# A graph attention layer on one core: packing the adjacency four columns to a word before it is searched

## The reference

```python
h = jnp.maximum(_layernorm(x, axis=-1), 0.0)
h = jnp.einsum('ni,hif->hnf', h, W)
s1 = jnp.einsum('hnf,hf->hn', h, a1)
s2 = jnp.einsum('hnf,hf->hn', h, a2)
scores = jax.nn.leaky_relu(s1[:, :, None] + s2[:, None, :], negative_slope=0.2)
scores = jnp.where(adj[None] > 0, scores, -9e15)
att = jax.nn.softmax(scores, axis=-1)
out = jnp.einsum('hnm,hmf->hnf', att, h)
x = x + elu(transpose and reshape of out to (6144, 512))
```

## Time and profile before

| | |
|---|---|
| median of 3 runs | 944.34 us (942.68 to 944.92) |
| profiled execution, its own time | 940.65 us |
| its span | 938.7 us |
| VectorE busy | 781.5 us, 83% |
| TensorE busy | 625.6 us, 67% |
| ScalarE busy | 467.2 us, 50% |
| GpSimd busy | 451.0 us, 48% |
| FIND_INDEX8, L327, 240 of them | 337.3 us |
| ACTIVATE of the adjacency, L430, 96 of them | 266.2 us |
| granted TensorE clock, mean | 0.853 |

### The profile page before, as it was taken

How to read it: one execution, slowest core, us unless ns; L and a number is a source line. 1 busy time by engine, 2 the same in 40 slices (tenths; PEclk the granted TensorE clock), 3 DMA queues, 4 the chain that set the end, 5 groups by cost and what they waited for, 6 DMA issues and landing times. The chain is left out here.

```text
span 938.7 us, 9287 instructions
## 1 busy us (share of the span) xinstructions
PE 625.6 (67%) x2178; PEld 363.9 (39%) x2178; DVE 781.5 (83%) x1767; ACT 467.2 (50%) x707; POOL 451.0 (48%) x1004
## 2 busy tenths in 40 slices
PE   0115766665766766657753695598957896978894
PEld 0003433433433434434432453355534453545442
DVE  3799999999989989989987675377958697989995
ACT  0217888888888888888881110012312231223322
POOL 3404444444444344344442666745767476746730
PEclk9967798899889889897895797789969798989897
DMA  8635999999999999999941666756868588868862
GB/s 290 236 134 194 395 402 414 413 414 418 415 413 419 414 411 413 415 415 408 407 157 47 192 183 170 228 155 199 241 208 266 167 262 258 261 211 255 278 218 91
DMA packets 86011, 269.53 MB, mean 287 GB/s; under 512 B 16129, under 2 KB 24321, under 8 KB 81218
## 3 DMA queue, kind: packets, MB, share of 16 engines
q1 hardware_dynamic: 66194, 203.13, 55.8%
q0 software_dynamic: 19760, 65.78, 24.0%
HBM read 243.49 MB, written 25.37 MB: 286 GB/s over the span
## 5 line engine op out<-in xcount | busy, mean ns | idle before, releaser
L327 DVE FIND_INDEX8 places<-ones,sb_adj_rows 128x8 uint32<-128x392 int32 (+6 forms) x240 | 337.3, 1413 | 0.0
L430 ACT ACTIVATE positive<-sb_adj_rows 128x3088 bf16<-128x3088 int32 (+3 forms) x96 | 266.2, 2773 | 0.0
L491 PE MATMUL psH<-sb_W,normedT 128*128 128x512 f32 x384 | 246.3, 734 | 1.7 <-ACT normedT L451 1.7
L1060 PE MATMUL psO<-weighted_h,ident 128*128 128x512 f32 x276 | 171.5, 710 | 25.1 <-issue 25.1
L832 POOL DMA_INDIRECT nodes<-table,column x138 | 140.8, 1020 | 66.1 <-issue 40.4
L483 PE MATMUL psT<-ident,normed 128*128 128x128 f32 x192 | 37.8, 329 | 199.7 <-ACT normed L444 199.7
L837 POOL DMA_INDIRECT nodes<-table,list_column x109 | 111.0, 1018 | 76.3 <-DVE list_column L945 45.0
L986 DVE TENSOR_TENSOR weighted_h<-nodes,psW 128x2048 f32<-128x2048 f32 (+5 forms) x74 | 139.5, 1925 | 0.0
L533 POOL TENSOR_TENSOR node_sum<-node_sum,h_rows 128x512 f32<-128x512 f32 x48 | 61.1, 1274 | 153.0 <-ACT h_rows L460 153.0
L1066 PE MATMUL psO<-weighted_h,to_row 128*128 128x512 f32 x218 | 127.0, 668 | 6.6 <-issue 4.4
L492 PEld LDWEIGHTS psS<-sb_Wa,normedT 128*128 128x128 f32 x384 | 84.6, 220 | 114.9 <-issue 114.9
(11 more groups left out here) (155 smaller groups left out, 852.7 us busy)
## 6 DMA issues: line engine op xcount, KB each, us to landing
sb_adj_rows<-in_adj_dram SPq DMA_DIRECT2D x36, 1344.0 KB, 13.4
sb_adj_rows<-in_adj_dram SPq DMA_DIRECT2D x36, 960.0 KB, 9.3
sb_adj_rows<-in_adj_dram SPq DMA_DIRECT2D x36, 576.0 KB, 6.6
table<-h_rows SPq DMA_DIRECT2D x48, 260.0 KB, 9.6
sb_x_rows<-in_x_dram SPq DMA_DIRECT2D x48, 256.0 KB, 9.8
x_part<-in_x_dram SPq DMA_DIRECT2D x19, 512.0 KB
out_dram<-result SPq DMA_DIRECT2D x19, 512.0 KB
sb_adj_rows<-in_adj_dram SPq DMA_DIRECT2D x10, 720.0 KB, 9.9
```

The costliest lines, as they stand in the source:

```text
L327: ins = nc.vector.max_index(places[:, t % 2, 8 * s:8 * s + 8], sb["ones"][:, 0:8], adj_rows[:, u, a:b + SENTINELS])
L430: ins = nc.scalar.activation(positive[:, cols], adj_rows[:, u, cols], ACT.Relu, accum_out=sb["sums"][:, t, half:half + 1])
L491: nc.tensor.matmul(psH[:, t % 2], normedT[:, t % 2, kc], sb["W"][:, kc], start=(kc == 0), stop=(kc == KC - 1))
L1060: nc.tensor.matmul(psO[:, o, i], sb["ident"][:], weighted_h[:, u % 2, q], start=a, stop=False)
```

## The change

ScalarE's pass over the adjacency writes something that is then used. The 6144 columns of a row are taken as four stretches of 1536 (WORDS). pack(t, b) writes stretch b as byte b of 1536 words (packed, two buffers), so a word holds columns w, 1536 + w, 3072 + w and 4608 + w. Byte 0 is written as 4 in place of 1, so that a word has an exact value in f32; the plan weighs its count by 0.25. VectorE then works on 1536 words a tile: greatest finds the eight greatest words of each segment (nc.vector.max, MAX8), search finds their places (max_index against these words), with 16, 8 or 4 segments as before. GpSimd takes the found words apart: for each of the four bytes it tests whether it is over 0 and makes the falling number of its column, so there are four times as many candidates, and rank works on arrays four times as wide. Sentinels, their memsets and the table of lengths are gone; a tile's adjacency is loaded in one DMA issue of whole rows. Its buffer is free when ScalarE has packed it.

VectorE's order for tile t is now moments(t + 2), scale(t + 1), greatest(t), then the searches of all segments with the ranks of t - 1 between them. greatest(t) waits for checked to reach t + 1, which the last pack of tile t sets. ScalarE's pack(t) waits, from tile 3 on, for the search of t - 2. The orders of ScalarE and GpSimd keep their places.

```diff
-SENTINELS = 8
+PACK = 4
+WORDS = N // PACK
...
 
-    marks = [N * k * k // (shares * shares) for k in range(shares + 1)]
+    def edges(w):
+        return sum(math.sqrt(b * WORDS + w) - math.sqrt(b * WORDS) for b in range(PACK))
+    marks = [0] + [min(range(WORDS + 1), key=lambda w: abs(edges(w) - edges(WORDS) * k / shares)) for k in range(1, shares)] + [WORDS]
...
-                for s, (lo, hi) in enumerate(segments):
-                    nc.gpsimd.memset(sb["lens"][t][:, 8 * s:8 * s + 8], float(hi - lo))
-                    nc.gpsimd.memset(sb["bases"][t][:, 8 * s:8 * s + 8], float(N + 1 - lo))
+                for b in range(PACK):
+                    for n, (lo, hi) in enumerate(segments):
+                        nc.gpsimd.memset(sb["bases"][t][:, b, 8 * n:8 * n + 8], float(N + 1 - lo - b * WORDS))
...
                 if t + AB < TILES:
-                    sp.wait_ge(searched, t + 1)
+                    if t == 0:
+                        sp.wait_ge(keyed, 1)
                     sp.wait_ge(checked, t + 1)
-                    load_adj(sp, sb, adj, t + AB)
+                    sp.dma_start(adj_rows[:, t % AB], adj[(t + AB) * P:(t + AB + 1) * P]).then_inc(adj_loaded[t % AB], 16)
...
-            def search(t, lo, hi):
-
-                u, where = t % AB, placed(t)
-                if lo == 0:
-                    dve.wait_ge(adj_loaded[u], adj_landed(t))
-                    dve.wait_ge(sentinels_set, sentinel_writes(t))
-                    if t >= 3:
-                        dve.wait_ge(cands_ready, t - 2)
-                for s in range(lo, hi):
-                    a, b = where[s]
-                    ins = nc.vector.max_index(places[:, t % 2, 8 * s:8 * s + 8], sb["ones"][:, 0:8],
-                                              adj_rows[:, u, a:b + SENTINELS])
-                if hi == len(where):
+            def segments_of(t):
+                return LAYOUTS[layout_of(t)]
+
+            def greatest(t):
+
+                dve.wait_ge(checked, t + 1)
+                if t >= 3:
+                    dve.wait_ge(cands_ready, t - 2)
+                for n, (lo, hi) in enumerate(segments_of(t)):
+                    ins = nc.vector.max(best[:, t % 2, 8 * n:8 * n + 8], packed[:, t % 2, lo:hi])
+                ins.then_inc(best_found, 1)
+
+            def search(t, n):
+
+                lo, hi = segments_of(t)[n]
+                dve.wait_ge(best_found, t)
+                ins = nc.vector.max_index(places[:, t % 2, 8 * n:8 * n + 8], best[:, t % 2, 8 * n:8 * n + 8], packed[:, t % 2, lo:hi])
+                if n == len(segments_of(t)) - 1:
                     ins.then_inc(searched, 1)
...
-                    first = 8 * next(s for s, seg in enumerate(LAYOUTS[layout_of(t)]) if seg[0] == v.lo)
-                    part = cands[:, t % 2, first:first + 8 * len(v.segments)]
+                    part = cands[:, t % 2, v.lo // WORDS * 8 * len(segments_of(t)):v.hi // WORDS * 8 * len(segments_of(t))]
...
-                dve.wait_ge(adj_loaded[0], adj_landed(0))
+                dve.wait_ge(adj_loaded[0], 16)
...
-                ins.then_inc(searched, 1)
+                ins.then_inc(keyed, 1)
...
-                segments = len(LAYOUTS[layout_of(t)])
+                segments = len(segments_of(t))
                 moments(t + 2)
-                search(t, 0, segments // 2)
                 scale(t + 1)
+                greatest(t)
                 done, left = 0, steps_of(t - 1) if t > 1 else 0
-                for s in range(segments // 2, segments):
-                    search(t, s, s + 1)
-                    upto = left * (s + 1 - segments // 2) // (segments - segments // 2)
-                    for n in range(done, upto):
-                        rank(t - 1, n)
+                for n in range(segments):
+                    search(t, n)
+                    upto = left * (n + 1) // segments
+                    for m in range(done, upto):
+                        rank(t - 1, m)
                     done = upto
             for n in range(steps_of(TILES - 1)):
                 rank(TILES - 1, n)
 
...
-            def check(t, half):
-
-                u, w = t % AB, width_of(t)
-                if half == 0:
-                    act.wait_ge(adj_loaded[u], adj_landed(t))
-                    act.wait_ge(sentinels_set, sentinel_writes(t))
-                    if t >= 1:
-                        act.wait_ge(checked, t)
-                cols = slice(0, w // 2) if half == 0 else slice(w // 2, w)
-                ins = nc.scalar.activation(positive[:, cols], adj_rows[:, u, cols], ACT.Relu, accum_out=sb["sums"][:, t, half:half + 1])
-                if half:
+            def pack(t, b):
+
+                u = t % AB
+                if b == 0:
+                    act.wait_ge(adj_loaded[u], 16 * (t // AB + 1))
+                    if t >= 3:
+                        act.wait_ge(searched, t - 2)
+                    if t == 2:
+                        act.wait_ge(checked, 1)
+                into = packed[:, t % 2].bitcast(mybir.dt.uint8).rearrange("p (w b) -> p b w", b=PACK)[:, b]
+                ins = nc.scalar.activation(into, adj_rows[:, u, b * WORDS:(b + 1) * WORDS], ACT.Relu, scale=4.0 if b == 0 else 1.0,
+                                           accum_out=sb["sums"][:, t, b:b + 1])
+                if b == PACK - 1:
                     ins.then_inc(checked, 1)
...
             for t in range(TILES):
                 turned(t)
                 norm(t + 1)
-                check(t, 0)
+                pack(t, 0)
+                pack(t, 1)
                 if t >= 1:
                     h_out(t - 1)
                 deviation(t + 2)
-                check(t, 1)
+                pack(t, 2)
+                pack(t, 3)
...
-            def sentinels(t):
-
-                if t < TILES and fresh_layout(t):
-                    if t >= AB:
-                        pool.wait_ge(searched, t - AB + 1)
-                        pool.wait_ge(checked, t - AB + 1)
-                    for _, b in placed(t):
-                        ins = nc.gpsimd.memset(adj_rows[:, t % AB, b:b + SENTINELS], 1)
-                    ins.then_inc(sentinels_set, 1)
-
             def candidates(t):
 
                 u, k = t % 2, layout_of(t)
                 w = 8 * len(LAYOUTS[k])
-                pool.wait_ge(searched, t + 1)
+                pool.wait_ge(searched, t)
                 if t >= 3:
                     pool.wait_ge(cut_step, cut_count(t - 1))
-                nc.gpsimd.tensor_copy(place[:, u, 0:w], places[:, u, 0:w]).then_inc(tested, 1)
-                pool.wait_ge(tested, 4 * t - 3)
-                nc.gpsimd.tensor_tensor(inside[:, u, 0:w], sb["lens"][k][:], place[:, u, 0:w], ALU.subtract).then_inc(tested, 1)
-                nc.gpsimd.tensor_tensor(falling[:, u, 0:w], sb["bases"][k][:], place[:, u, 0:w], ALU.subtract).then_inc(tested, 1)
-                pool.wait_ge(tested, 4 * t - 1)
-                nc.gpsimd.tensor_scalar(inside[:, u, 0:w], inside[:, u, 0:w], 0.0, None, ALU.is_gt).then_inc(tested, 1)
-                pool.wait_ge(tested, 4 * t)
                 if t <= 2:
                     pool.wait_ge(crowd_done, 8)
-                nc.gpsimd.tensor_tensor(cands[:, u, 0:w], inside[:, u, 0:w], falling[:, u, 0:w], ALU.mult).then_inc(cands_ready, 1)
-            for t in range(1, AB):
-                sentinels(t)
+
+                def by_byte(array):
+                    return array[:, 0:PACK * w].rearrange("p (b w) -> p b w", b=PACK)
+                nc.gpsimd.tensor_copy(found_words[:, u, 0:w], best[:, u, 0:w]).then_inc(tested, 1)
+                nc.gpsimd.tensor_copy(place[:, u, 0:w], places[:, u, 0:w]).then_inc(tested, 1)
+                pool.wait_ge(tested, 4 * t - 2)
+                nc.gpsimd.tensor_scalar(by_byte(there), found_words[:, u, 0:w].bitcast(mybir.dt.uint8).rearrange("p (w b) -> p b w", b=PACK),
+                                        0.0, None, ALU.is_gt).then_inc(tested, 1)
+                nc.gpsimd.tensor_tensor(by_byte(falling), sb["bases"][k][:], place[:, u, 0:w].unsqueeze(1).to_broadcast([P, PACK, w]),
+                                        ALU.subtract).then_inc(tested, 1)
+                pool.wait_ge(tested, 4 * t)
+                nc.gpsimd.tensor_tensor(cands[:, u, 0:PACK * w], there[:, 0:PACK * w], falling[:, 0:PACK * w], ALU.mult).then_inc(cands_ready, 1)
             spread(0)
             offset(0)
             spread(1)
```

In the plan:

```diff
             did(nc.vector.tensor_reduce(most[:, H:2 * H], S2(sb).rearrange("p t h -> p h t"), AX.X, ALU.min))
-            did(nc.vector.tensor_reduce(in_rows[:], sb["sums"][:], AX.X, ALU.add))
+            did(nc.vector.tensor_reduce(last_rows[:], sb["sums"][:, :, 1:PACK], AX.X, ALU.add))
...
             dve.wait_ge(filled, 1)
+            did(nc.vector.scalar_tensor_tensor(in_rows[:], sb["sums"][:, :, 0], 0.25, last_rows[:], ALU.mult, ALU.add))
             did(nc.vector.tensor_tensor(listed[:], degree[:], taken[:], ALU.subtract))
...
 
```

(41 more changed lines are left out.)

11 lines of the change are left out of this document (4 added, 7 removed).

## The result

The changed kernel takes 1307.96 us (median of four runs, 1302.91 to 1310.87) against 943.51 us for the kernel before (942.37 to 944.92): the ratio is 1.387, 95% interval 1.383 to 1.391. It is slower by 364.5 us. The profiled execution of the changed kernel has a span of 1307.5 us.

The account below looks back on a forecast made before the run. Transfers were taken to bound late tiles, with VectorE nearly tied in early ones; after the change, engines taking turns: 2.1 + 0.5 + 7.5 + 0.1 + 4.6 = 14.8 us a late tile, + 298 us in all, 1242 us, range 1190 to 1310.

Parts of the forecast that it names:

- The ring's own range: Spread of the closed engine cycle: 23 us either way for casts and handoffs, start 5, comparison 28: 1205 to 1290.
- three signs that I had set for being wrong: Packs of t start before search(t-1) ends, a pack takes over 2 us, or late period outside 14 to 16 us.
- for latencies that no row shows: Widening of the range on both sides, from 1205 to 1290 out to 1190 to 1310 us.
- The new wait: VectorE's greatest(t) waits for all packs, so engines take turns: late period 14.8 us against 8.84; chance 0.85.
- GpSimd's part: Candidates, then scaled and shift, between VectorE's search and ScalarE's normed: 2.1 us a late tile, 3.1 an early one.
- VectorE's part: MAX8, search and rank steps behind the packs: 4.6 us a late tile, 6.4 an early one.
- That rival: VectorE's MAX8 reads int32 at half rate: 1.6 us a tile more, 1317 us; chance 0.04.
- ScalarE's part: normed, four packs at 1.47 us, h_out and deviation: 7.5 us a turn, strided byte stores costing nothing extra.
- ScalarE pays double: Strided byte stores in ScalarE's packs double the element time: 5.1 us a turn, 1477 us; chance 0.05.
- The start: Fewer SyncE load issues in the set-up bring the first moments to 22 us, gaining 5.0 us.
- The edges: More than eight words in a segment would run the dense branch, well over 1500 us; fullest counted 7; chance 0.02.
- The open ring: Reciprocal of t+1 reaches GpSimd before VectorE waits for packs, so packs run ahead: 937 us; chance 0.04.

Follow-up runs that it names:

- e3: Kernel before with scale(t + 1) moved ahead of the whole search of t and a wait for ScalarE's check between them, no packing: 1231.76 us, ratio 1.403.
- e2: Changed kernel with moments and scale issued one tile earlier on VectorE, offset and spread following on GpSimd: 897.51 us, ratio 1.023 to the kernel before.
- e6: Changed kernel with four neighbouring columns per word, bytes written side by side in two passes, same order: 1154.74 us, ratio 1.314 to the kernel before.
- e4: Changed kernel with GpSimd's candidates(t - 1) moved behind offset(t + 1): 1185.04 us, ratio 1.349 to the kernel before.
- e1: Changed kernel plus twelve ScalarE passes behind its scan, writing the same input in six forms, with and without accumulator: 1249.31 us in one execution.

## Why the prediction held, and where it was off

The direction, the cause and the place were right; 1242 us was forecast and 1308 measured, 66 us more. That is 2 us inside the stated range, and one of the four executions, at 1310.87, lies outside it. The ring's own range, 1205 to 1290, missed it (its terms, 23 us either way, 5 for the start and 28 for the comparison, add up to 1214 to 1298), and one of the three signs that I had set for being wrong did come: the late period is 16.23 us, outside 14 to 16. So the mechanism held, and the size came in by luck: by the margin "for latencies that no row shows", which was spent on something else, the price of the packs. Read off the ends of the searches, 48.8 of the 66 us lie in the 34 late turns (16.2 us each, forecast 14.8), 12.5 in nine early ones (18.9, forecast 17.5) and the rest in the start and in tiles 1, 2, 12 and 47. The steps:

**The new wait** closed a ring, as predicted. Forecast for a late turn: ScalarE waits some 6.5 us for shift (measured 6.64), VectorE some 9 us for the packs (10.74, 1.5 of the surplus being the dearer packs), VectorE busy some 40% (5.46 of 16.23, 34%). e3 shows that the wait with this order suffices by itself, e2 that without it the loss is 19.0 us.

**GpSimd's part** was 2.1 us and is 2.0 (500.93 to 502.93); the comparison on bytes takes 0.53 us where I took 0.56, and 0.53 too in e6, where the bytes are read side by side, so reading bytes with a step cost nothing extra. e4 shows the link, 1.0 us a late turn.

**VectorE's part**: MAX8 on int32 runs at the rate of f32, four of them in 1.94 us against 1.95. That rival is out.

**ScalarE's part** is the term that was mis-sized. A pack is 1.85 us from start to start and not 1.47. Four of them make 1.5 us a turn, and over 46 turns and tile 47 that is 71 us, where the whole miss is 66. The nearest row, the same function on the same input, wrote contiguous bf16 and said nothing about the store. The ceiling I had set, twice the element time, held it: the surcharge is 0.38 of 1.28 us. This is a part of the rival that ScalarE pays double; it had 5.1 us a turn and it is 1.5. The Trainium skill, SBUF — State Buffer, "Door 1: The DMA port swizzle", which I had cited for a free store, differs from e1 here: four of these bytes do fall in one 16-byte line, and they cost 0.25 ns each all the same. The measurement decides.

**The start** came out: first moments at 21.75, forecast 22. The first moments of tile 1's turn start at 63.23, forecast 64.1.

**The edges** hold in their eight words: what follows the scan is nearly as long as before (457.0 us, 452.2 before), so the dense branch did not run.

**The open ring** as a rival didn't occur: in the changed kernel no pack of a tile starts before the search of the tile before is over, but for tile 47, whose packs start at 837.4 where the search of tile 46 ends at 841.8; the forecast had that exception. The Trainium skill, TensorE: Matmul & The Clock Gate, "Architectural detail", with its strict order on ScalarE, VectorE and GpSimd, agrees with this: the reciprocal never left ahead of the MAX8 that waited, and it took an edit of the order (e2) to get it there.

**The sum** with the measured pack: 1242 + 71 = 1313 us, 5 over the measured time. The start, 0.9 us earlier than counted, and GpSimd's part, 0.1 us a turn shorter, are of that size.

## What to carry to other kernels

When an operation starts to read what another engine makes in the same round, write down for each engine what stands ahead of that hand-over in its queue, and follow it back. If the path comes round to the waiting engine's own last step, the period is the sum of the engines' parts, whatever else each engine has time for. Then the second buffer doesn't help, and every part counts in full, also that of an engine which is mostly idle: the packs without the step gave 85 us (e6), and the order of GpSimd's candidates 55 (e4). Issuing the small early step (here a reciprocal of one column) one round ahead opens the ring, and it was worth 342 us. Then read a price from a row with the same *output* pattern as well as the same input, or measure it before it goes into every round.

## What the runs showed of the hardware

In e1 ScalarE writes narrow elements with a 4-byte step at 1.08 ns an element (1.85 us per 1536 less 0.19) and the other forms at 0.83, bytes with a step of 2 included.

The durations that the profile shows for ScalarE then lag: in e1, behind packs of tile 47, a read of the accumulator is shown at 0.44 to 0.51 us, in the kernel before mostly at 0.19, while the starts stay as close as ever. Behind strided stores one should read ScalarE's time from start to start. Whether the lag is a queue of writes was not tested; in the changed kernel it grows within a turn (a pack from 1.91 to 1.99 us) and is gone after the wait. In e2, where ScalarE does not wait, a pack is shown at 2.44 to 2.49 us and a read of the accumulator at 0.67 to 0.75, with starts still 1.86 us apart.

Between chips the changed kernel's scan took the same time (its last search ends at 850.5, 849.7 and 849.9 us on the three), and what follows it did not: 457.0 us on the first and 388.0 on the third. The work is the same (VectorE is busy 340.9 and 340.8 us behind the scan) and the waits are longer; on the first chip ScalarE's facts (L854) wait 120.8 us in all for what the profile calls remote, another core or an unknown queue, a wait that the third chip's trace doesn't show, and TensorE's granted clock is 0.82 against 0.89. Why was not tested.
